# Router logits by column tiles: a batch's four tiles side by side in the array instead of one 512-column product

## The chip, the cores and the metric

The kernel is one program on one core of a Trainium2 chip. It runs four pairs of layers (a cross-attention and a feed-forward layer each) over 4 batches of 512 tokens with 256 features. The metric is the device time of one execution in microseconds (us), from runs of the whole program.

## The reference, cut to what matters

Three of the eight layers are mixtures of experts (layer 0, layer 1 and layer 3). Each begins in the same way: the tokens are normalised, multiplied by a small router matrix, and the two largest of 8 (in layer 1: 7) logits name the token's experts.

```python
x = x + _L0_ffn_ref(_layernorm(x, axis=-1), L0_ffn_router_w, ...)
...
scores = jnp.einsum('btd,de->bte', x, router_w).astype(jnp.float32)      # layer 0: 256 -> 8
probs = jax.nn.softmax(scores, axis=-1)
routing_weights, routing_idx = jax.lax.top_k(probs, TOP_K)
...
logits = xt @ W_router + routing_bias                                    # layer 1: 256 -> 7
probs = jax.nn.sigmoid(logits)
...
logits = xf @ Wg                                                         # layer 3: 256 -> 8
top_w, top_i = jax.lax.top_k(logits, TOP_K)
```

The expert products that follow (gate, up, down for every token and its two experts) are by far the larger work, and the change does not touch them.

## The kernel before, in words

**Names.** P is 128, a tile is 128 tokens, T is 16 tiles, B is 4 batches of TB = 4 tiles (S = 512 tokens). KC = 2 is the number of 128-row pieces of the 256 features. The three expert layers carry the tags e0, e1 and e3.

**Stages.** The program is a row of blocks. In a block each engine has its own queue of instructions, written in the order in which it runs; semaphores order the engines among each other. A block ends for all engines together: nobody begins the next block before the slowest has come to its end, the queue of SyncE (SP) that issues DMAs among them. `experts` opens with two blocks, `normalise` (tags e0n, e1n, e3n) and `route` (e0r, e1r, e3r), and then runs the expert blocks (e0b, e1b, e3b).

**normalise.** VectorE makes mean and inverse deviation of all 16 tiles and then writes the 16 normalised tiles `xn` one after the other (L380; in e1 L383). TensorE turns each tile into a PSUM buffer `tp` of which there are four (L428, two transposes a tile), and ScalarE copies it to `xnT` (L402). Between them stand the router's products. `logits(b)` waits until ScalarE has copied the four tiles of batch b (`copied`), and from b = 2 on until VectorE has copied the logits of batch b - 2 (`lt_copied`), since the PSUM tile `lt` has two buffers. It holds the router's weights (128 x 8) in the array and streams 512 tokens through, once for each of the two pieces of features (L412). In fp32 the profile shows two records for one such product. The order on TensorE is: five filler products, tiles 0 to 5, `logits(0)`, tiles 6 to 9, `logits(1)`, tiles 10 to 13, `logits(2)`, tiles 14 and 15, `logits(3)`, and then `turn_logits` for the four batches (L419). VectorE copies `lt` to `lts` (L390), but those four copies stand behind all 16 `xn` tiles in its queue. `turn_logits(b)` turns 8 x 128 logits for each of the four tiles into `lp`, where tokens lie on the partitions.

**Beside it in the same block.** SP issues loads and stores (`early`, L339): in e0 and e3 the start value of `y_sum` and two pieces of the down weights, in e0 also the rows of a later layer's weights (`rows.load`, L2645 to L2648); in e1 three small matrices.

**route.** It begins with VectorE's copy of `lp` to `lg` (L2040; in e1 an addition of the bias), the search for the two largest (L2043, L2046), and a chain of small operations up to the table `token` (L2158). SP first stores `xn` to `x_rows` (L1976). In e0 the down weights have a left-over half chunk, so POOL clears a part of `xn` (L1818) once two stores of `xn` have landed. In e1 the shared expert's products run on TensorE beside the chain (L1843, L1867), and ScalarE's first silu (L1876) waits for the store of `xn`, whose room it writes. TensorE has filler products (`stay_busy`, L308), 20 and 44 of them in e0 and e3, and 30 at the start of the expert blocks e0b and e3b.

Of the kernel before, what the change touches and what calls it, by code (L numbers as in the profile page):

```python
# [125 lines left out]
def build(nc, ctx, ins, out):  # L126
    def sb(name, shape, dt=F32):
        return ctx.enter_context(nc.sbuf_tensor(name, shape, dt))
# [43 lines left out]
    def matrix(name, n_in, n_out):  # L172
        t = sb(f"w_{name}", [P, n_in // P, n_out])
        loads.append((t[:], ins[name].rearrange("(k p) n -> p k n", p=P)))
        return t
# [50 lines left out]
    for h in range(HC):  # L226
        at = h % 4 * 2 * HD + h // 4 * HD
        loads.append((w.o1[at:at + HD, :, :], o1_rows[h * HD:(h + 1) * HD]))
    w.router = [matrix("L0_ffn_router_w", D, NE), matrix("L1_ffn_W_router", D, NE - 1), matrix("L3_ffn_Wg", D, NE)]
    w.rbias = spread("L1_ffn_routing_bias", NE - 1)  # L230

    w.fm = sb("fm_diag", [P, P])
# [4 lines left out]

    with ExitStack() as st:
        sem = Semaphores(nc, st, "p")
        loaded, made, tr_done, tr_copied, prep = (sem(n) for n in (  # L240
            "loaded", "made", "tr", "trc", "prep"))
        x_in = [sem(f"x{b}") for b in range(B)]
        fm_rows = st.enter_context(nc.sbuf_tensor("fm_rows", [P, HD], F32))
        tp = st.enter_context(nc.psum_tensor("ctx_tp", [P, KC, B * L], F32))
# [1 line left out]
        with nc.Block() as block:  # L246
            FIRST = 6

            @block.sync
            def _(sp):  # L250
                for b in range(B):
                    sp.dma_start(x[:, b * TB:(b + 1) * TB, :], ins["x"][b].rearrange("(t p) d -> p t d", p=P)).then_inc(x_in[b], 16)
                sp.dma_start(consts[:], ins["consts"]).then_inc(loaded, 16)
                sp.dma_start(ctx_load[:], ins["ctx_1024"].rearrange("b l d -> (b l) d")
                             .rearrange("(k p) d -> p k d", p=P)).then_inc(loaded, 16)
                sp.dma_start(ctx_tok[:], ins["ctx_1024"].rearrange("b l d -> l b d")).then_inc(loaded, 16)
                sp.dma_start(w.fmb_row[:], ins["L1_xattn_fm_b"].partition_broadcast(P)).then_inc(loaded, 16)
                sp.dma_start(fm_rows[:], ins["L1_xattn_fm_wT"]).then_inc(loaded, 16)
                sp.dma_start(w.fmb[:], ins["L1_xattn_fm_b8"]).then_inc(loaded, 16)

                for dst, src in loads[0:first_loads]:
                    sp.dma_start(dst, src).then_inc(weights_loaded[0], 16)

            @block.vector
            def _(dve):
# [44 lines left out]
    def normalise(tag, x, xn, rms_weight=None, router=None, stats=None, stats_of_xn=None, arriving=None, early=(), rows=None):  # L310
# [6 lines left out]
        with ExitStack() as st:  # L317
# [8 lines left out]
            idle = st.enter_context(nc.psum_tensor(f"{tag}_idle", [P, S], F32))  # L326
            if router is not None:
                lp, wr, E = router
                lt = [st.enter_context(nc.psum_tensor(f"{tag}_lt{j}", [E, S], F32)) for j in range(2)]
                lts = st.enter_context(nc.sbuf_tensor(f"{tag}_lts", [E, B, S], F32))  # L330
                lt_made, lt_copied = sem("lt_made"), sem("lt_copied")
            with nc.Block() as block:
                if arriving is not None or early:
# [71 lines left out]
                def _(pe):  # L405
                    def logits(b):

                        pe.wait_ge(copied, (b + 1) * TB)
                        if b >= 2:
                            pe.wait_ge(lt_copied, b - 1)  # L410
                        for k in range(KC):
                            last = nc.tensor.matmul(lt[b % 2][:], wr[:, k, :], xnT[:, k, b * S:(b + 1) * S],  # L412
                                                    start=(k == 0), stop=(k == KC - 1))
                        last.then_inc(lt_made, 1)

                    def turn_logits(b):
                        pe.wait_ge(lt_copied, b + 1)
                        for t in range(TB):
                            nc.tensor.transpose(lp[:, b * TB + t, 0:E], lts[:, b, t * P:(t + 1) * P], ident[0:E, 0:E])  # L419

                    if stats_of_xn is None:
                        stay_busy(idle[:], 5 if stats is not None else 16)
# [1315 lines left out]
    def experts(tag, layer, x, wr, w_gate, w_up, w_down, F, rms_weight=None, shared=None, bias=None, outer=None,  # L1738
# [14 lines left out]
        with ExitStack() as st:  # L1753
# [7 lines left out]
            if shared:  # L1761
                NB = (TOP * B * S + E * (P - 1)) // P
                with ExitStack() as s2:
# [6 lines left out]
                    with ExitStack() as s3:  # L1770
                        beside_route = SharedExpert(s3, f"{tag}s", *shared, F, into, fills, kept)
                        with ExitStack() as s4:
                            lp = s4.enter_context(nc.psum_tensor(f"{tag}_lp", [P, T, NE], F32))
                            normalise(f"{tag}n", x, xn, rms_weight, (lp, wr, E), st6, early=beside_route.weights)
                            route(tag, lp, E, wt, slot, owner, token, bias, x, outer, beside_route)
                    kept_blocks(tag, kept_gu, kept_d, (kept, 16 * len(fills[0] + fills[1])), F, NB, E, owner, token)
            else:
                plan = SummedBlocks(st, tag, x, w_down, F, E)
                with ExitStack() as s2:
                    lp = s2.enter_context(nc.psum_tensor(f"{tag}_lp", [P, T, NE], F32))  # L1780
                    normalise(f"{tag}n", x, xn, rms_weight, (lp, wr, E), st6, early=plan.early, rows=beside)
                    route(tag, lp, E, wt, slot, owner, token, bias, x, outer, plan=plan)
                blocks(tag, w_gate, w_up, F, NB, E, owner, token, plan, beside, result)
# [110 lines left out]
    def route(tag, lp, E, wt, slot, owner, token, bias, x, outer, beside=None, plan=None):  # L1894
# [5 lines left out]
        with ExitStack() as st:  # L1900
# [35 lines left out]
            with nc.Block() as block:  # L1936
# [94 lines left out]
                def _(dve):  # L2031
# [4 lines left out]
                    if bias is not None:  # L2036
                        nc.vector.tensor_tensor(lb[:, :, 0:E], lp[:, :, 0:E], bcast(bias[:], 1, T), ALU.add).then_inc(lg_done, 1)
                        dve.wait_ge(prob_done, 1)
                    else:
                        nc.vector.tensor_copy(lg[:], lp[:]).then_inc(lg_done, 1)  # L2040
                        dve.wait_ge(lg_done, 1)
                    for t in range(T):
                        nc.vector.max(m8[:, t, :], lg[:, t, :]).then_inc(max_done, 1)  # L2043
# [1133 lines left out]
```

## Time and profile before

| what | value |
|---|---|
| median of 3 runs | 1805.71 us (1800.82 to 1808.09) |
| the profiled execution's own time | 1800.69 us |
| its span, first to last instruction | 1798.8 us |
| granted TensorE clock, mean over the span | 0.946 of full speed |
| block e0n, from VectorE's first instruction to SP's first in route | 133.2 to 150.9 us |
| block e1n | 934.1 to 951.6 us |
| block e3n | 1474.3 to 1492.1 us |

A row of a time line reads: start, length of the group from its first start to its last end, engine, line, operation, what it writes and reads, shapes, count, and in brackets how long the engine was idle before it and who released it. PE is TensorE, PEld its weight loads, DVE VectorE, ACT ScalarE, POOL GpSimd, SPq the queue that issues DMAs. A matmul record's length holds the time to drain, so records of a stream overlap.

### The profile page before, as it was taken

Reading aid. Unit: us, or ns where it says so; the run is one execution under the profiler, and the core shown is the slowest. Engines: PE = TensorE matmul, PEld = TensorE weight load, DVE = VectorE, ACT = ScalarE, POOL = GpSimd, SP = SyncE. Lnnn points to the kernel's source line nnn. Section 1 sums busy time; section 2 is a strip of 40 time slices with the busy share of each in tenths; the row PEclk is TensorE's granted clock in tenths of the full one; section 3 lists DMA queues with packets and bytes.
Section 4 is the critical chain, followed back from the end, with each engine's and each line's share of the span. In section 5 each row is a group of like instructions: output and inputs, shape, how many; then the busy total and the mean of one; then the engine's idle time right before and its main releaser. Section 6 shows DMA issues by size and latency. Waiting matters only on the chain. (4 is left out here: it accounts for less than half of the span.)

```text
span 1798.8 us, 33336 instructions
## 1 busy us (share of the span) xinstructions
PE 1550.2 (86%) x11830; PEld 1155.5 (64%) x11831; DVE 958.4 (53%) x2462; ACT 487.2 (27%) x1029; POOL 486.0 (27%) x594
## 2 busy tenths in 40 slices
PE   5887999999979986999979899578897888988885
PEld 3653899999858742455444566346665654878785
DVE  4455244444359866766556333689885464222221
ACT  2331111011067531455621122223322431000000
POOL 0101344444400001111102343422120102455543
PEclk9998999999969998999999999788998998999998
DMA  4108677777510017244115133200000025666665
GB/s 142 40 8 277 221 226 223 218 212 222 154 50 2 2 36 194 61 108 111 52 32 170 50 88 82 62 24 13 1 1 1 2 62 189 206 200 201 200 182 140
DMA packets 128641, 200.84 MB, mean 112 GB/s; under 512 B 20368, under 2 KB 77968, under 8 KB 128336
## 3 DMA queue, kind: packets, MB, share of 16 engines
q1 hardware_dynamic: 107696, 169.65, 29.3%
q0 software_dynamic: 20832, 29.68, 8.4%
q8 instruction: 71, 1.16, 0.3%
q14 instruction: 42, 0.34, 0.1%
HBM read 166.21 MB, written 35.16 MB: 112 GB/s over the span
## 5 line engine op out<-in xcount | busy, mean ns | idle before, releaser
L1528 DVE TENSOR_REDUCE l1a_nm<-l1a_sc 128x1 f32<-128x512 f32 (+3 forms) x256 | 107.1, 482 | 53.7 <-PE l1a_sc L1664 53.7
L2271 PEld LDWEIGHTS e0b_gp<-e0b_xT,e0b_wgu 128*128 128x128 f32 x936 | 110.5, 192 | 4.2 <-issue 1.5
L2271 PE MATMUL e0b_gp<-e0b_xT,e0b_wgu 128*128 128x128 f32 x936 | 111.0, 275 | 1.9 <-DVE e0b_hT L2350 1.4
L2331 ACT ACTIVATE e0b_sg<-e0b_gp 128x640 f32<-128x640 f32 x78 | 33.5, 481 | 270.9 <-PE e0b_gp L2271 270.9
L2242 POOL DMA_INDIRECT y_sum<-e0b_yb,e_token x39 | 63.5, 1628 | 145.6 <-DVE e0b_yb L2358 142.5
L2271 PE MATMUL e0b_up<-e0b_xT,e0b_wgu 128*128 128x128 f32 x780 | 93.5, 275 | 0.0
L2242 POOL DMA_INDIRECT y_sum<-e3b_yb,e_token x39 | 63.0, 1617 | 102.2 <-DVE e3b_yb L2358 99.3
L2271 PEld LDWEIGHTS e0b_up<-e0b_xT,e0b_wgu 128*128 128x128 f32 x780 | 90.2, 192 | 0.0
L2331 ACT ACTIVATE e3b_sg<-e3b_gp 128x512 f32<-128x512 f32 x39 | 23.3, 597 | 236.2 <-PE e3b_gp L2271 236.2
L2271 PE MATMUL e3b_up<-e3b_xT,e3b_wgu 128*128 128x128 f32 x624 | 80.3, 285 | 0.0
L2271 PEld LDWEIGHTS e3b_gp<-e3b_xT,e3b_wgu 128*128 128x128 f32 x624 | 75.6, 192 | 3.5 <-issue 0.9
L2271 PE MATMUL e3b_gp<-e3b_xT,e3b_wgu 128*128 128x128 f32 x624 | 76.1, 275 | 1.0 <-DVE e3b_xT L2343 0.5
L2271 PEld LDWEIGHTS e3b_up<-e3b_xT,e3b_wgu 128*128 128x128 f32 x624 | 76.9, 201 | 0.0
L1662 PE MATMUL l1a_sc<-l_stack_k,l_stack_q 128*128 128x512 bf16 (+3 forms) x256 | 59.1, 309 | 16.9 <-PEq L1310 15.2
L2438 PE MATMUL e1b_gu<-e_kgu,e1b_xT 128*128 x152 | 71.7, 594 | 1.7 <-DVE e1b_xT L2502 1.7
L2343 DVE COPY e3b_xT<-e3b_xp 128x256 f32<-128x256 f32 x39 | 16.5, 424 | 95.4 <-PE e3b_xp L2265 95.4
L1662 PEld LDWEIGHTS l1a_sc<-l_stack_k,l_stack_q 128*128 128x128 bf16 x256 | 25.3, 99 | 61.0 <-issue 27.1
L2350 DVE TENSOR_TENSOR e0b_hT<-e0b_up,e0b_sg 128x640 f32<-128x640 f32 x39 | 32.1, 824 | 57.6 <-PE e0b_up L2271 57.6
L1417 POOL TENSOR_TENSOR xn<-xn 128x512 f32<-128x512 f32 x8 | 10.1, 1260 | 194.9 <-DVE xn L1372 183.4
L2350 DVE TENSOR_TENSOR e3b_hT<-e3b_up,e3b_sg 128x512 f32<-128x512 f32 x39 | 27.0, 691 | 61.8 <-PE e3b_up L2271 61.8
L2594 POOL TENSOR_TENSOR f_hq<-f_q,f_q 128x704 f32<-128x704 f32 x16 | 22.9, 1433 | 136.8 <-DVE f_q L2581 136.8
L1191 DVE TENSOR_REDUCE a_nm<-a_sc 128x8 f32<-128x512 f32 x64 | 39.7, 682 | 36.3 <-PE a_sc L1041 36.3
(619 smaller groups left out, 3755.9 us busy)
## 6 DMA issues: line engine op xcount, KB each, us to landing
e3b_wgu<-in_L_ffn_W SPq DMA_DIRECT2D x78, 512.0 KB, 4.6
e0b_wgu<-in_L_ffn_gate_proj SPq DMA_DIRECT2D x39, 704.0 KB, 4.3
e0b_wgu<-in_L_ffn_up_proj SPq DMA_DIRECT2D x39, 704.0 KB, 5.6
x_rows<-xn SPq DMA_DIRECT2D x3, 2048.0 KB, 8.6
l_parts<-l1p_split SPq DMA_DIRECT2D x16, 384.0 KB, 3.1
l_stack_k<-l_parts SPq DMA_DIRECT2D x48, 128.0 KB, 2.7
l_stack_q<-l_parts SPq DMA_DIRECT2D x48, 128.0 KB, 3.0
y_slots<-e1b_yb SPq DMA_DIRECT2D x38, 128.0 KB
```

Of the source, the lines that this page charges most:

```text
L1191: nc.vector.tensor_reduce(nm[:, :, r, :], bank[r][:].rearrange("p t (h l) -> p t h l", l=L), AX_X, ALU.max, negate=True).then_inc(max_done, 1)
L1417: nc.gpsimd.tensor_tensor(whole[n], t1[n], t2[n], ALU.add).then_inc(done, 1)
L1528: nc.vector.tensor_reduce(nm[:, g % 2, q, i:i + 1], sc[q], AX_X, ALU.max, negate=True).then_inc(max_done, 1)
L1662: nc.tensor.matmul(sc[q], of_head(1, n)[:, q * P:(q + 1) * P], of_head(0, n)[:, 0:(q + 1) * P], start=True, stop=False)
L2242: pool.indirect_dma_start(y_sum, bass.IndirectOffsetOnAxis(ap=token[:, n:n + 1], axis=0), yb[n % 2][:], None, compute_op=ALU.add).then_inc ...
L2271: last = nc.tensor.matmul(dst[:, f, :], wgu[j][:, k, at + f * P:at + (f + 1) * P], xT[j][:, k, :], start=(k == 0), stop=(k == KC - 1))
L2331: last = nc.scalar.activation(sg[rows, chunks, :], gp[rows, chunks, :], ACT.Silu)
L2343: nc.vector.tensor_copy(xT[j][:], xp[:]).then_inc(x_copied, 1)
L2350: last = nc.vector.tensor_tensor(hT[j][rows, chunks, :], from_up, sg[rows, chunks, :], ALU.mult)
L2438: last = nc.tensor.matmul(gu[n % 2][:], xT[n % 2][:, k, :], wgu[:, bass.ds(e, 1), k, :].rearrange("p a f -> p (a f)"), start=(k == 0), sto ...
L2594: nc.gpsimd.tensor_tensor(v3(dst), v3(a[:, 0:n]), bcast(sc[:, 0:n // FP4_BLOCK], 2, FP4_BLOCK), ALU.mult).then_inc(result, 1)
```

## The change

The router's weights lie in tiles of 32 columns, whose columns 8 to 31 (7 to 31 in layer 1) are cleared once by POOL in the program's first block. `logits(b)` gives each of the batch's four tiles a column group of the array of its own: for each piece of features, four products of 128 x 32 weights by 128 tokens, which write 32 partitions each of one PSUM tile [128, 128]. VectorE's copy is then 128 x 128 instead of 8 x 512, and one transpose turns all four tiles of a batch. `lp` is 32 columns wide for a tile, and `route` reads the first 8 (7).

```diff
-    w.router = [matrix("L0_ffn_router_w", D, NE), matrix("L1_ffn_W_router", D, NE - 1), matrix("L3_ffn_Wg", D, NE)]
+    ROUTER = P // TB
+    w.router = []
+    for name, n_out in (("L0_ffn_router_w", NE), ("L1_ffn_W_router", NE - 1), ("L3_ffn_Wg", NE)):
+        w.router.append(sb(f"w_{name}", [P, KC, ROUTER]))
+        loads.append((w.router[-1][:, :, 0:n_out], ins[name].rearrange("(k p) n -> p k n", p=P)))
...
+            @block.gpsimd
+            def _(pool):
+                for router in w.router:
+                    nc.gpsimd.memset(router[:], 0.0).then_inc(cleared, 1)
+                pool.wait_ge(cleared, len(w.router))
...
-                lt = [st.enter_context(nc.psum_tensor(f"{tag}_lt{j}", [E, S], F32)) for j in range(2)]
-                lts = st.enter_context(nc.sbuf_tensor(f"{tag}_lts", [E, B, S], F32))
+                lt = [st.enter_context(nc.psum_tensor(f"{tag}_lt{j}", [P, P], F32)) for j in range(2)]
+                lts = st.enter_context(nc.sbuf_tensor(f"{tag}_lts", [P, B, P], F32))
...
                         for k in range(KC):
-                            last = nc.tensor.matmul(lt[b % 2][:], wr[:, k, :], xnT[:, k, b * S:(b + 1) * S],
-                                                    start=(k == 0), stop=(k == KC - 1))
+                            for t in range(TB):
+                                at = (b * TB + t) * P
+                                last = nc.tensor.matmul(lt[b % 2][t * ROUTER:(t + 1) * ROUTER, :], wr[:, k, :], xnT[:, k, at:at + P],
+                                                        start=(k == 0), stop=(k == KC - 1))
                         last.then_inc(lt_made, 1)
...
-                        for t in range(TB):
-                            nc.tensor.transpose(lp[:, b * TB + t, 0:E], lts[:, b, t * P:(t + 1) * P], ident[0:E, 0:E])
+                        nc.tensor.transpose(lp[:, b * TB:(b + 1) * TB, :].rearrange("p t e -> p (t e)"), lts[:, b, :], ident)
...
-                            lp = s4.enter_context(nc.psum_tensor(f"{tag}_lp", [P, T, NE], F32))
+                            lp = s4.enter_context(nc.psum_tensor(f"{tag}_lp", [P, T, ROUTER], F32))
...
-                        nc.vector.tensor_copy(lg[:], lp[:]).then_inc(lg_done, 1)
+                        nc.vector.tensor_copy(lg[:], lp[:, :, 0:NE]).then_inc(lg_done, 1)
```

On TensorE, in the block e3n (e0n and e1n read alike), the queue of before holds these rows; `e3n_tp` are the turned tiles, `e3n_lt` the logits with the experts on the partitions, `e_lp` those with the tokens on the partitions. A row counts products here, not the profile's records.

```order
L308 MATMUL e3n_idle<-ones_h,ident_h 128x512 x5
L428 MATMUL e3n_tp<-consts,xn 128x128 x12
L412 MATMUL e3n_lt<-xnT,w_L_ffn_Wg 8x512 x2
L428 MATMUL e3n_tp<-consts,xn 128x128 x8
L412 MATMUL e3n_lt<-xnT,w_L_ffn_Wg 8x512 x2
L428 MATMUL e3n_tp<-consts,xn 128x128 x8
L412 MATMUL e3n_lt<-xnT,w_L_ffn_Wg 8x512 x2
L428 MATMUL e3n_tp<-consts,xn 128x128 x4
L412 MATMUL e3n_lt<-xnT,w_L_ffn_Wg 8x512 x2
L419 MATMUL e_lp<-consts,e3n_lts 128x8 x16
```

The same place in the queue of the changed kernel (its lines are numbered some ten higher):

```order
L318 MATMUL e3n_idle<-ones_h,ident_h 128x512 x5
L439 MATMUL e3n_tp<-consts,xn 128x128 x12
L424 MATMUL e3n_lt<-xnT,w_L_ffn_Wg 32x128 x8
L439 MATMUL e3n_tp<-consts,xn 128x128 x8
L424 MATMUL e3n_lt<-xnT,w_L_ffn_Wg 32x128 x8
L439 MATMUL e3n_tp<-consts,xn 128x128 x8
L424 MATMUL e3n_lt<-xnT,w_L_ffn_Wg 32x128 x8
L439 MATMUL e3n_tp<-consts,xn 128x128 x4
L424 MATMUL e3n_lt<-xnT,w_L_ffn_Wg 32x128 x8
L430 MATMUL e_lp<-consts,e3n_lts 128x128 x4
```

Nothing has moved in the order: each group of 2 products with 512 columns has become 8 with 128 columns on 32 partitions, and the 16 small transposes at the end are 4 full ones.

On VectorE, at the end of the same block and the start of route, the queue of before holds:

```order
L376 RECIPROCAL e3n_rstd<-e3n_root 128x16
L380 TENSOR_SCALAR xn<-x,e3n_mean,e3n_rstd 128x256 x16
L390 COPY e3n_lts<-e3n_lt 8x512 x4
L332 UNCONDITIONAL_BRANCH
L2030 UNCONDITIONAL_BRANCH
L2033 MEMSET e3k_weight_of 128x2
L2040 COPY e3r_lg<-e_lp 128x128
```

and in the changed kernel:

```order
L386 RECIPROCAL e3n_rstd<-e3n_root 128x16
L390 TENSOR_SCALAR xn<-x,e3n_mean,e3n_rstd 128x256 x16
L400 COPY e3n_lts<-e3n_lt 128x128 x4
L342 UNCONDITIONAL_BRANCH
L2041 UNCONDITIONAL_BRANCH
L2044 MEMSET e3k_weight_of 128x2
L2051 COPY e3r_lg<-e_lp 128x128
```

The four copies of the logits keep their place behind the 16 tiles of `xn`; only their shape is another.

## Rows read from the trace of the kernel before

**Rows 1.** The page: busy time of each engine, and POOL in 40 slices.

```profile
PE 1550.2 (86%) x11830; PEld 1155.5 (64%) x11831; DVE 958.4 (53%) x2462; ACT 487.2 (27%) x1029; POOL 486.0 (27%) x594
...
POOL 0101344444400001111102343422120102455543
```

**Rows 2.** Time line of block e3n: start, us, engine, line.

```profile
1476.25 5.25 DVE L380 TENSOR_SCALAR xn<-x,e3n_mean,e3n_rstd 128x256 f32<-128x256 f32 x16
1476.71 2.82 PE L428 MATMUL e3n_tp<-consts,xn 128*128 128x128 f32 x12 [1.09 <-DVE xn L380]
...
1479.46 2.19 PE L412 MATMUL e3n_lt<-xnT,w_L_ffn_Wg 128*8 128x512 f32 x4
...
1485.75 1.88 PE L412 MATMUL e3n_lt<-xnT,w_L_ffn_Wg 128*8 128x512 f32 x4
...
1487.57 0.66 PE L428 MATMUL e3n_tp<-consts,xn 128*128 128x128 f32 x4
...
1488.74 1.88 PE L412 MATMUL e3n_lt<-xnT,w_L_ffn_Wg 128*8 128x512 f32 x4 [0.52 <-ACT xnT L402]
...
1490.56 1.25 PE L419 MATMUL e_lp<-consts,e3n_lts 8*128 8x8 f32 x16
1490.66 0.68 DVE L390 COPY e3n_lts<-e3n_lt 8x512 f32<-8x512 f32 x1 [2.31 <-PE e3n_lt L412]
1492.06 0.37 SPq L1976 DMA_DIRECT2D x_rows<-xn  x1
```

**Rows 3.** Time line of block e1n.

```profile
936.42 6.42 DVE L383 SCALAR_TENSOR_TENSOR xn<-inner,e1n_rstd,s_L_ffn_w_ln 128x256 f32<-128x256 f32 x16
...
947.15 0.66 PE L428 MATMUL e1n_tp<-consts,xn 128*128 128x128 f32 x4
...
948.33 1.88 PE L412 MATMUL e1n_lt<-xnT,w_L_ffn_W_router 128*7 128x512 f32 x4 [0.52 <-ACT xnT L402]
...
951.64 0.37 SPq L1976 DMA_DIRECT2D x_rows<-xn  x1
```

**Rows 4.** Time line of TensorE in layer 0's attention, 66 to 72 us.

```profile
68.09 1.17 PE L1041 MATMUL a_sc<-a_kd,a_qT 32*128 32x128 f32 x32
69.20 1.07 PE L1075 MATMUL a_ob<-a_pT,a_vd 128*32 128x256 f32 x16
70.09 1.06 PE L1083 MATMUL a_rb<-a_pT,consts 128*32 128x128 f32 x32
```

**Rows 5.** Stretches of e0n and e0r: busy time, granted clock, DMA share, GB/s.

```profile
145.00:148.00 3.00, 2.48 (x9) 0.69 (x8) 0.68 (x1) 0.76 (x3) 0.00 (x0) 1.00 1.09 350
...
163.00:166.00 3.00, 3.00 (x16) 1.37 (x14) 3.00 (x2) 0.00 (x0) 0.00 (x0) 1.00 1.09 347
```

**Rows 6.** SP's queue around the end of block e0n.

```profile
148.32 0.37 SPq L2648 DMA_DIRECT2D f2w_rows<-in_L_ffn_w_down  x1
150.91 0.37 SPq L1976 DMA_DIRECT2D x_rows<-xn  x1
```

**Rows 7.** Waits of e0n and e0r, the longest.

```profile
POOL xn L1818 <- DMA x_rows<-xn: 32.5, 1, 32.5
```

**Rows 8.** Time line of e3r and the start of e3b.

```profile
1492.14 0.29 DVE L2040 COPY e3r_lg<-e_lp 128x128 f32<-128x128 f32 x1
...
1497.96 9.66 PE L308 MATMUL e3r_idle<-ones_h,ident_h 128*128 128x512 bf16 x44
...
1514.85 0.18 DVE L2158 CAST e_token<-e3r_row_f 128x39 uint32<-128x39 f32 x1
...
1515.34 9.46 PE L308 MATMUL e3b_gp<-ones_h,ident_h 128*128 128x512 bf16 x30 [1.74 <-PEq L1936]
```

**Rows 9.** A stretch of e3r, with columns as in rows 5.

```profile
1507.00:1510.00 3.00, 0.62 (x3) 0.10 (x1) 3.00 (x2) 0.00 (x0) 3.00 (x2) 1.00 0.01 4
```

**Rows 10.** Time line of TensorE in e1r: products of the shared expert.

```profile
955.20 3.60 PE L1843 MATMUL e1s_up<-xnT,e1s_wu 128*128 128x512 f32 x8
961.32 5.37 PE L1843 MATMUL e1s_gp<-xnT,e1s_wg 128*128 128x512 f32 x8 [2.52 <-ACT xn L1876]
```

More of the change, by code:

```diff
@@ L239, in build @@
         sem = Semaphores(nc, st, "p")
-        loaded, made, tr_done, tr_copied, prep = (sem(n) for n in (
-            "loaded", "made", "tr", "trc", "prep"))
+        loaded, made, tr_done, tr_copied, prep, cleared = (sem(n) for n in (
+            "loaded", "made", "tr", "trc", "prep", "cleared"))
         x_in = [sem(f"x{b}") for b in range(B)]
@@ L1779, in experts @@
                 with ExitStack() as s2:
-                    lp = s2.enter_context(nc.psum_tensor(f"{tag}_lp", [P, T, NE], F32))
+                    lp = s2.enter_context(nc.psum_tensor(f"{tag}_lp", [P, T, ROUTER], F32))
                     normalise(f"{tag}n", x, xn, rms_weight, (lp, wr, E), st6, early=plan.early, rows=beside)
```

## The prediction

> **What bounds the kernel now.** I read the page first: TensorE is busy 86% of the span and no other engine over 53% [rows 1]. That is a mean over stages, so it says little about three blocks of under 18 us each. The time line of a block says more, and the reader is to follow who waits for whom in it.
>
> In e3n VectorE is through with its 16 tiles at 1476.25 + 5.25 = 1481.50, but the block ends at 1492.06. Behind VectorE the block is a chain of TensorE and ScalarE with one period a batch: from `logits(2)` (1485.75) to the next transposes (1487.57) 1.82 us, from there to `logits(3)` (1488.74) 1.17 us, which is two tiles turned and copied by ScalarE. Then comes a tail: products 1.88 us, VectorE's copy 0.68 us from 1490.66 to 1491.34, and 0.72 us of the last transposes and the end of the block [rows 2]. e1n runs in the same way, only that its `xn` tiles take 6.42 us, up to 942.84 [rows 3].
>
> e0n looks the same on TensorE, but two other things happen there. SP issues its last DMA of the block at 148.32 and is done at 148.69, 2.2 us ahead of the block's end [rows 6]; and the DMA engines are full, share 1.09, in a stretch inside e0n and in one 18 us later in e0r [rows 5]. What e0r waits for in the end is a landing: POOL stands 32.5 us until the stores of `xn` have landed [rows 7].
>
> **What the new products cost.** The trace of before holds the nearly exact form: L1083, 128 x 32 weights by 128 columns in fp32, four column groups in turn, 32 records in 1.06 us [rows 4]. A batch's logits are now 8 products, 16 records. Half of 1.06 is 0.53 us; with the last record's drain, which does not halve, I take 0.60 us until the next work of another form starts and 0.65 us until VectorE has the result. The bounds: below, 0.53; above, no overlap of the groups at all, which leaves the 1.82 us of before, since the same columns stream. I stay near the lower end, for the row differs from the new products only in its operands. The 64 weight loads a stage instead of 16 are inside that row, since it has one for each record too.
>
> Changing between full and column-tiled products happens eight times a stage. The row: L1041 uses the array as four row groups, starts at 68.09 and runs 1.17 us, to 69.26; L1075, in column groups, starts at 69.20 [rows 4]. So a change of form waits for hardly more than the last record, and 0.60 holds that. The Trainium skill (TensorEngine Tiling (Array Packing), Key Properties) says that changing the mode drains the array; by that rule, read as a start 0.06 us later at each of 8 changes, a stage would lose 0.5 us more, the sum would be 9.4 us and the time 1796.3; the row does not show that extra.
>
> VectorE's copy: 8 x 512 takes 0.68 us [rows 2], and a 128 x 128 copy out of PSUM takes 0.29 us [rows 8]. The bounds are these two; I take 0.29, as it is the same form, a gain of 0.39 us, which counts once a stage, for the last batch. Turning: three of the four transposes are done while VectorE copies the last batch, and one is left instead of four small ones. Of the 0.72 us after the copy I let 0.1 go.
>
> **e3n.** Three times 1.82 - 0.60, once 1.88 - 0.65, then 0.39 and 0.1: 3.66 + 1.23 + 0.49 = 5.4 us. The first `logits` took 2.19 instead of 1.88 us at a clock not yet up [rows 2]; the new ones meet the same clock, so I book nothing there. Does VectorE become the bound? `logits(2)` needs the copy of batch 0, which comes at 1481.50 + 0.29 = 1481.8. TensorE reaches it at about 1479.46 + 2 x (0.6 + 1.17) + 0.3 = 1483.3, later, so no. After the block VectorE's chain in route ends at 1514.85 + 0.18 and the next block starts at 1515.34 [rows 8]; the DMA engines are idle in 1507 to 1510, share 0.01 [rows 9], so the stores landed early enough to move 5.4 us forward. e3n pays in full.
>
> **e1n.** Here VectorE is later. Last `xn` tile 942.84, copy of batch 0 to 943.13, `logits(2)` from 943.2 to 943.8, transposes to `logits(3)` 948.33 - 947.15 = 1.18 us, so 944.98; then 0.65 for products, 0.35 for the copy with its handover, 0.6 for the turn and the end: 946.6 instead of 951.64 [rows 3]. The gain is 5.0 us. In e1r TensorE is the bound apart from one wait of 2.52 us before its second gate product, which hangs on the store of `xn` [rows 10], and that store is the first DMA of the block, so it moves too.
>
> **e0n.** The block could end 2.2 us earlier, where SP stands. But the two stores of `xn`, behind which POOL waits, stand in a full DMA queue whose bytes are the same and which was full before and after [rows 5, 7]. They land when they did. I take 0; the other bound is the 2.2 us.
>
> **The rest.** POOL's three fills of 128 x 64 lie in the first slice of the program, where POOL has nothing to do (digit 0) [rows 1]; uncovered, at the 0.29 us of a copy of 128 elements [rows 8], they would be 0.9 us. `route` reads `lp` with gaps instead of in one piece, 128 elements in both cases, so its 0.29 us [rows 8] stay. SP's loads of the routers are the same pieces.
>
> **Sum.** 5.0 + 5.4 + 0 = 10.4 us. The profiled execution took 1800.69 us, so it would take 1790.3. That execution is near the lowest of the runs shown, whose median is 1805.71, and I forecast the median: 1795.3 us.
>
> **Rivals.**
> - *The clock takes a part back.* e3b opens with 30 filler products that took 9.46 us, while 44 of the same took 9.66 us in e3r [rows 8], so 0.22 us each at full clock and, at half, 0.44. Those 30 could take 6.6 us or 13.1 us, depending on when the clock rises. If the earlier start meets the worse case, 3.6 us go: gain 6.8, time 1798.9. For it: nothing sets when the clock rises but TensorE's activity, and that shifts. Against: the better case, 2.9 us more gain, is as open; both are in the own range.
> - *e0n pays too*: 2.2 us more, 12.6, time 1793.1. For it: the block's end is visibly TensorE's. Against: the share of 1.09.
> - *The column groups do not overlap here*, as the accumulation over two pieces might make each wait. Then only copy and turn are left, 0.5 us in each of two stages: 1.0, time 1804.7. Against: L1083 adds up four products in one place of PSUM as well, and keeps its pace [rows 4].
> - *The other side, slower: TensorE stays at half clock* through e1n and e3n and into the next stages, because the new products keep it less busy. Twelve transposes took 2.82 us at the low clock, so 1.9 us for eight; with 1.2 us for logits and 0.3 of ScalarE a batch takes 3.4 us instead of 2.99. The stage gains nothing and loses 1 us with the tail, twice 1.0; in e1r gate and up at half clock cost 2 x 3.60 less the wait of 2.52 [rows 10], 4.7 us; the filler 3.6 us. Together 10.3 us slower, 1816.0. It decides once the low clock lasts through the tail of both stages, which takes all 10.4 us of gain. Against: in e3n the low clock ended by itself under transposes alone, before the second batch, and eight transposes in every 1.8 us keep the array at work for most of it. The Trainium skill (TensorE: Matmul & The Clock Gate, Part 1) says that the throttled state is the default and activity lifts it; that would speak for this rival only if the array stood still for long, and no row of e3n shows that.
>
> **Chances and range.** Forecast 0.58; clock takes back 0.17; e0n pays 0.10; no overlap 0.10; slower 0.05. A difference of 0.5%, 9.0 us, is about what a measurement of this kernel tells from no change, so the line is 1796.7 us, close to the forecast. Of the forecast's case two thirds lie below it, of the second a sixth, of the third nearly all: 0.39 + 0.03 + 0.10 = 0.52 faster. Slower by over 0.5% is most of the last rival, 0.04; the rest, 0.44, is the same. The likeliest case's own range is 1791 to 1799 (the filler either way). The range for all is 1788.5 to 1803: it takes in the first three cases and the spread of the runs before, and leaves out the last two.
>
> **What would show it.** Right: L424's 16 records a batch within 0.7 us; e3n ends 5 to 6 us after its last `xn` tile instead of 10.6, e1n under 4 us after instead of 8.8; VectorE's copies 0.29 us; POOL's L1818 ends its wait at the same distance from the block's start. Wrong, if the logits' records follow each other at over 0.1 us, if the granted clock in 937 to 947 or after 1480 falls to 0.5, if the span from e3n's end to the first expert product grows, or if e0's POOL wait ends earlier.

## The result, and the profile after

| what | before | changed |
|---|---|---|
| median, runs on one chip | 1800.86 us (1799.31 to 1808.09, 5 runs) | 1788.0 us (1782.94 to 1790.93, 5 runs) |
| ratio, with its 95% interval | | 0.9911 (0.9882 to 0.9940) |
| the profiled execution's span | 1798.8 us | 1789.0 us |
| e0n / e0r | 17.5 / 28.2 us | 15.6 / 29.7 us |
| e1n / e1r | 17.5 / 49.9 us | 13.3 / 48.2 us |
| e3n / e3r | 17.5 / 23.2 us | 12.0 / 22.3 us |
| e3b, from its first product to the issue of the last store of the result | 274.6 us | 274.4 us |

The change is faster by 0.9%: 0.0089 x 1800.86 = 16.0 us, 10.8 to 21.3 by the interval. That ratio is worked out from all runs and is not the ratio of the two medians, which differ by 12.9 us. The forecast was 10.4 us and 1795.3 us; the measured median, 1788.0 us, is 0.5 us below its range of 1788.5 to 1803. A block is counted here between the same early instruction of it and of the next one (the first that touches `e0n_m`, `e0r_idle` and so on), so e0n and e3n come out some 0.25 us shorter than from first instruction to first.

In the page of the changed kernel TensorE has 15.1 us less to do than in [rows 1], and its share of the span is the same.

```profile
PE 1535.1 (86%) x11938; PEld 1155.7 (65%) x11939; DVE 954.2 (53%) x2462; ACT 487.7 (27%) x1029; POOL 487.1 (27%) x597
```

**e3n**, time line of the changed kernel, to be held against [rows 2]:

```profile
1473.34 5.26 DVE L390 TENSOR_SCALAR xn<-x,e3n_mean,e3n_rstd 128x256 f32<-128x256 f32 x16
1473.80 2.82 PE L439 MATMUL e3n_tp<-consts,xn 128*128 128x128 f32 x12 [1.10 <-DVE xn L390]
...
1476.55 0.92 PE L424 MATMUL e3n_lt<-xnT,w_L_ffn_Wg 128*32 128x128 f32 x16
...
1480.33 0.64 PE L424 MATMUL e3n_lt<-xnT,w_L_ffn_Wg 128*32 128x128 f32 x16
...
1480.90 0.66 PE L439 MATMUL e3n_tp<-consts,xn 128*128 128x128 f32 x4
...
1482.08 0.64 PE L424 MATMUL e3n_lt<-xnT,w_L_ffn_Wg 128*32 128x128 f32 x16 [0.52 <-ACT xnT L412]
...
1482.65 0.81 PE L430 MATMUL e_lp<-consts,e3n_lts 128*128 128x128 f32 x4
1482.79 0.29 DVE L400 COPY e3n_lts<-e3n_lt 128x128 f32<-128x128 f32 x1 [1.46 <-PE e3n_lt L424]
...
1483.72 0.37 SPq L1987 DMA_DIRECT2D x_rows<-xn  x1
```

The 16 records of a batch take 0.64 us where 1.88 stood, and the next transposes start 0.57 us after the first of them (1480.33 to 1480.90). VectorE's copy is 0.29 us instead of 0.68, and SP's first store of route comes 1483.72 - 1478.60 = 5.12 us after the last `xn` tile, where it was 10.56.

**e1n**, against [rows 3]:

```profile
939.04 6.42 DVE L393 SCALAR_TENSOR_TENSOR xn<-inner,e1n_rstd,s_L_ffn_w_ln 128x256 f32<-128x256 f32 x16
...
942.25 1.08 PE L424 MATMUL e1n_lt<-xnT,w_L_ffn_W_router 128*32 128x128 f32 x16
...
943.27 1.77 PE L439 MATMUL e1n_tp<-consts,xn 128*128 128x128 f32 x8
...
944.97 0.64 PE L424 MATMUL e1n_lt<-xnT,w_L_ffn_W_router 128*32 128x128 f32 x16
...
946.71 0.64 PE L424 MATMUL e1n_lt<-xnT,w_L_ffn_W_router 128*32 128x128 f32 x16
...
950.10 0.37 SPq L1987 DMA_DIRECT2D x_rows<-xn  x1
```

Here eight transposes take 1.77 us instead of 1.09, and the first logits 1.08 instead of 0.64: the granted clock is low in the first two batches, at 0.50 (1.2 GHz) in these 2 us:

```profile
942.00:944.00 2.00, 2.00 (x22) 1.33 (x21) 2.00 (x6) 0.69 (x3) 0.00 (x0) 0.50 0.04 8
```

The prediction had named a clock of 0.5 in this place as a sign of being wrong. It did come, and it is not the change's doing alone: the kernel before has it in some of its profiles too (below, `before_again`). The block ends 4.64 us after the last `xn` tile (939.04 + 6.42 = 945.46), not under 4 as forecast.

**e1r.** TensorE's time line behind that block, against [rows 10], and the granted clock of 3 us in which the second gate product begins, in the changed kernel:

```profile
953.65 3.60 PE L1854 MATMUL e1s_up<-xnT,e1s_wu 128*128 128x512 f32 x8
959.80 3.70 PE L1854 MATMUL e1s_gp<-xnT,e1s_wg 128*128 128x512 f32 x8 [2.55 <-ACT xn L1887]
```

```profile
core 0: us, PE busy (x) PEld busy (x) DVE busy (x) ACT busy (x) POOL busy (x), PEclk, DMA share, GB/s
959.00:962.00 3.00, 2.20 (x5) 1.06 (x6) 2.86 (x10) 0.75 (x2) 0.47 (x1) 1.00 1.09 365
```

and the same place in the kernel before:

```profile
961.00:964.00 3.00, 2.68 (x3) 1.18 (x4) 2.70 (x10) 0.26 (x1) 0.02 (x1) 0.55 1.09 361
```

The wait is the same, 2.55 and 2.52 us. The eight records behind it take 3.70 us at a clock of 1.00, 2.4 GHz, where they took 5.37 with 0.55 granted, nearly all of it the lower level. That is 1.67 us of gain in a block that the change does not touch.

**e3r** has the same thing in small. The last products of its chain, in the changed kernel and then before:

```profile
1503.01 1.30 PE L1977 MATMUL e3r_small<-e3r_numbers,e3r_place_hot 128*128 128x78 bf16 x32 [3.73 <-DVE e3r_numbers L2137]
```

```profile
1511.34 2.26 PE L1966 MATMUL e3r_small<-e3r_numbers,e3r_place_hot 128*128 128x78 bf16 x32 [3.72 <-DVE e3r_numbers L2126]
```

0.96 us less behind a wait of the same length. The granted clock around these products, in the changed kernel and then before:

```profile
1503.00:1504.00 1.00, 0.99 (x28) 0.99 (x29) 0.00 (x0) 0.00 (x0) 0.00 (x0) 1.00 0.00 0
1504.00:1505.00 1.00, 0.31 (x9) 0.17 (x5) 0.65 (x7) 0.00 (x0) 0.00 (x0) 0.74 0.00 0
```

```profile
1510.00:1511.00 1.00, 0.00 (x0) 0.00 (x0) 1.00 (x2) 0.00 (x0) 0.49 (x1) 0.92 0.00 0
1511.00:1512.00 1.00, 0.66 (x11) 0.66 (x12) 0.28 (x1) 0.00 (x0) 0.00 (x0) 0.50 0.00 0
```

In the kernel before the clock has fallen when the products begin. In the changed kernel it falls as well, but only when they are nearly done: the fall was moved, not avoided.

**e0.** SP's queue around the end of e0n and POOL's wait, against [rows 6, 7]:

```profile
148.91 0.37 SPq L2659 DMA_DIRECT2D f2w_rows<-in_L_ffn_w_down  x1
149.68 0.37 SPq L1987 DMA_DIRECT2D x_rows<-xn  x1
```

```profile
POOL xn L1829 <- DMA x_rows<-xn: 32.1, 1, 32.1
```

The block now ends where SP is done and is 1.9 us shorter, and e0r takes 1.5 us more: given back, as forecast. POOL's wait ends 35.4 us behind SP's first instruction of e0n before (168.57 - 133.16) and 35.1 us behind it now (168.96 - 133.85).

### The profile page after: what moved, and what is told of

It is laid out like the page before. It is cut to its first block and busy times, and to the rows that moved or that the text cites. A ratio compares the mean times of both kernels' runs of the same rounds, so it can differ in the third digit from the quotient of the medians.

```text
span 1789.0 us, 33557 instructions
## 1 busy us (share of the span) xinstructions
PE 1535.1 (86%) x11938; PEld 1155.7 (65%) x11939; DVE 954.2 (53%) x2462; ACT 487.7 (27%) x1029; POOL 487.1 (27%) x597
## 5 line engine op out<-in xcount | busy, mean ns | idle before, releaser
L1202 DVE TENSOR_REDUCE a_nm<-a_sc 128x8 f32<-128x512 f32 x64 | 39.8, 684 | 37.1 <-PE a_sc L1052 37.1
```

Of the source, the lines that this page charges most:

```text
L1202: nc.vector.tensor_reduce(nm[:, :, r, :], bank[r][:].rearrange("p t (h l) -> p t h l", l=L), AX_X, ALU.max, negate=True).then_inc(max_done, 1)
```

## The experiments

Each ratio is against the kernel before on the same chip (17 or 23 runs of it, medians 1803.73 to 1803.95 us). It comes from all runs, so it can differ from the ratio of the medians by up to 0.0013 (`one_group`). The gain is (1 - ratio) x 1803.9, with its interval. "Blocks" is what one profile of the kernel shows in the six blocks, e0n, e0r, e1n, e1r, e3n and e3r, against the mean of the profiles with untiled products in that stage: e0n + e0r 45.8 us, e1n 18.3, e1r 50.1, e3n 17.4, e3r 23.2. Those means are from six or seven profiles each. The mean of e1r holds the 51.6 us of `one_group`; the other five lie at 49.7 to 49.9.

| kernel | median us | ratio (interval) | gain us | blocks us |
|---|---|---|---|---|
| `again` | 1787.84 | 0.9905 (0.9885 to 0.9924) | 17.1 (13.7 to 20.7) | 14.2 |
| `only_e0` | 1799.83 | 0.9983 (0.9968 to 0.9997) | 3.1 (0.5 to 5.8) | 0.4 |
| `only_e1` | 1792.51 | 0.9941 (0.9922 to 0.9960) | 10.6 (7.2 to 14.1) | 7.2 |
| `only_e3` | 1790.98 | 0.9931 (0.9913 to 0.9949) | 12.4 (9.2 to 15.7) | 6.9 |
| `one_group` | 1804.92 | 0.9994 (0.9979 to 1.0008) | 1.1 (-1.4 to 3.8) | -2.3 |
| `two_groups` | 1794.88 | 0.9959 (0.9941 to 0.9976) | 7.4 (4.3 to 10.6) | 7.8 |
| `moved_before` | 1807.83 | 1.0012 (0.9999 to 1.0026) | -2.2 (-4.7 to 0.2) | 0.4 |
| `moved_after` | 1787.45 | 0.9900 (0.9880 to 0.9919) | 18.0 (14.6 to 21.6) | 19.9 |
| `before_fill` | 1802.30 | 0.9992 (0.9977 to 1.0008) | 1.4 (-1.4 to 4.1) | 2.5 |
| `early_copy` | 1787.65 | 0.9922 (0.9894 to 0.9949) | 14.1 (9.2 to 19.1) | 14.9 |
| `best` | 1784.18 | 0.9891 (0.9864 to 0.9919) | 19.7 (14.6 to 24.5) | 20.8 |

**The change once more (`again`), and the tiles in one layer alone.** The theory: the gain is made of e1n and e3n with what lies right behind them, and e0 pays nothing. The rival: e0 pays too, or there is a gain elsewhere. `only_e1`, `only_e0` and `only_e3` differ in the list:

```diff
+                tiled = tag in ['e1n']
...
+                        for k in range(KC if not tiled else 0):
+                            last = nc.tensor.matmul(lt[b % 2][:], wr[:, k, 0:E], xnT[:, k, b * S:(b + 1) * S],
+                                                    start=(k == 0), stop=(k == KC - 1))
+                        for k in range(KC if tiled else 0):
```

> The changed kernel once more, beside new runs of the kernel before. Theory A (the change is worth the 9.6 us that the two profiles show in e1 and e3, the rest of the measured difference is the chance of when TensorE's clock rises): 9 to 12 us faster, ratio near 0.994. Theory B (there is a further gain that the profiles of one run each did not show): 14 to 18 us faster, ratio near 0.991, as before.

> Column tiles in layer 0's router alone, layers 1 and 3 as before (with the padded weights read in 8 columns). Theory A: no gain, within 1 us, since the stores of xn in e0 wait in a full DMA queue; the block e0n ends where SP does, near 15.8 us after its start. Theory B: 2 to 5 us faster, if the shorter block is worth something after all.

> Column tiles in layer 1's router alone. Theory A: 5.0 us faster (the block e1n 13.4 to 12.5 us long instead of 17.5, and all of it passed on). Theory B: more than 5, since e1r is bound by TensorE and may find a higher clock: 6 to 8 us.

> Column tiles in layer 3's router alone. Theory A: 5.4 us faster (block e3n 12.3 us instead of 17.7). Theory B: more, through e3r and the fillers at the start of e3b, 7 to 9 us.

e1n goes to 13.3 us and e1r to 48.2 in `only_e1`, and e1r is at 49.7 and 49.9 in the other two; e3n goes to 12.0 and e3r to 22.3 in `only_e3` and in neither of the other two. So each effect sits behind its own stage. `only_e0` has e0n + e0r at 45.2 us, a gain of 0.6, though its runs put it at 3.1 us (0.5 to 5.8). By the runs all four came out above the theory A of their expectation, and `only_e1` and `only_e3` above theory B as well, while the blocks of `only_e1` and `only_e3` (7.2 and 6.9 us) are near what their theory B named, a gain in e1r and e3r. The three gains add to 26.1 us, and the whole change gives 17.1. Part of this is that the three share one measurement of the kernel before, part is the stage at the end. Granted clock over the 240 us that begin 10 us after e3b's start, in the kernel before, in `again` and in `only_e3`:

```profile
1525.30:1765.30 240.00, 208.75 (x1530) 197.85 (x1531) 57.69 (x109) 22.09 (x37) 126.01 (x107) 0.98 0.67 196
```

```profile
1516.90:1756.90 240.00, 209.84 (x1562) 198.72 (x1563) 58.73 (x110) 22.09 (x37) 127.10 (x108) 0.99 0.69 199
```

```profile
1520.50:1760.50 240.00, 211.37 (x1586) 200.27 (x1587) 59.85 (x112) 22.69 (x38) 129.09 (x109) 1.00 0.69 202
```

From e3b to the end these took 274.6, 270.2 and 268.9 us. Over all fourteen profiles this stretch lies between 268.9 and 275.5 us: 272.3 to 275.5 (mean 274.5) for the five kernels without overlapping groups in any layer, 270.2 to 275.2 (mean 272.2) for the five with four groups in all three, 272.8, 269.2 and 268.9 in `only_e0`, `only_e1` and `only_e3`, and 275.4 in `two_groups`. So a single profile is uncertain by some 3 us here. The first pair of profiles differed by only 9.8 us, although their six blocks differ by 12.7, and this stretch is not the reason. What stands ahead of e3b outside the six blocks, which the change does not touch, took 1361.5 us in the first profile of the kernel before, the least of all fourteen, and 1364.9 in the changed kernel (1368.7 in `moved_before`). The pair was unlucky for the change there; its own profiled execution was the slowest of five. Whether the tiles move this clock a little on the average is open; even the lower end of the interval of `only_e3` is 2.3 us above what its blocks explain.

**A second profile of the kernel before (`before_again`)**, without a change.

> The kernel before once more, for a second profile of it. Theory A+ (part of the gain is in stretches behind the changed blocks, at TensorE's clock): the gate product of e1r behind the wait for the store takes 5.2 to 5.4 us again and the last products of e3r 2.3 us, as in the three profiles with an unchanged block there, and the expert blocks e3b take 270 to 280 us at random. Rival (those were chance): the two durations differ from profile to profile.

```profile
940.23 2.73 PE L428 MATMUL e1n_tp<-consts,xn 128*128 128x128 f32 x12 [1.59 <-DVE xn L383]
942.88 3.13 PE L412 MATMUL e1n_lt<-xnT,w_L_ffn_W_router 128*7 128x512 f32 x4
```

The first logits took 3.13 us instead of 1.88 and e1n 19.0 instead of 17.5. The product in e1r behind the wait took 5.26 us and the last ones of e3r 2.26, as theory A+ had it. Its time was 1802.68 us, its e3b stretch 272.3. Over seven profiles with untiled e1n that block took 17.5 (three times), 18.7, 18.9, 19.0 and 19.2 us: the block which the prediction read was at the lucky end.

**All products on one column group (`one_group`).** The theory: the gain is the overlap of the groups. The rival: padding or shorter products bring it. The edit also runs tile by tile, with the two pieces of features inside, and makes `lt` and `lts` 32 x 512:

```diff
...
-                                last = nc.tensor.matmul(lt[b % 2][t * ROUTER:(t + 1) * ROUTER, :], wr[:, k, :], xnT[:, k, at:at + P],
+                                last = nc.tensor.matmul(lt[b % 2][:, t * P:(t + 1) * P], wr[:, k, :], xnT[:, k, at:at + P],
...
-                        nc.tensor.transpose(lp[:, b * TB:(b + 1) * TB, :].rearrange("p t e -> p (t e)"), lts[:, b, :], ident)
+                        for t in range(TB):
+                            nc.tensor.transpose(lp[:, b * TB + t, :], lts[:, b, t * P:(t + 1) * P], ident[0:ROUTER, 0:ROUTER])
```

> The same 128 x 32 by 128 products as in the change, with the same padded weights, but all four tiles of a batch on the same 32 columns of the array, one after the other; copy is 32 x 512 and four transposes turn a batch. Theory A (the gain is the overlap of the four column groups): no overlap, a batch's logits take 1.8 us again and the time is that of before, 0 to 2 us slower. Rival (shorter products or narrower weights are what pays): 8 us or more faster, as the change.

```profile
1488.37 1.93 PE L424 MATMUL e3n_lt<-xnT,w_L_ffn_Wg 128*32 128x128 f32 x16
1490.24 1.09 PE L440 MATMUL e3n_tp<-consts,xn 128*128 128x128 f32 x8
```

The same 16 records take 1.93 us, and the next transposes start 1.87 us behind the first of them; e3n is at 17.4 us and by the runs there is no gain. Padding and shorter products bring nothing. VectorE's copy is 0.68 us again here (32 x 512), so the run does not part the overlap from the smaller copy, which comes with it; by the rows the copy is 0.39 us of the 5.4, and the rest is the overlap and one transpose instead of four. (The -2.3 us in the column of blocks are the clock in this one profile, in e1n with 19.2 us and in e1r with 51.6.)

**Two column groups (`two_groups`)** asks whether the gain is in proportion. The `lt` and `lts` tiles are 64 x 256 in it.

```diff
...
-                            for t in range(TB):
-                                at = (b * TB + t) * P
+                        for u in range(2):
+                            for k in range(KC):
+                                for g in range(2):
+                                    at = (b * TB + u * 2 + g) * P
...
```

> The batch's four tiles on two column groups instead of four, two tiles after each other in each; the copy is 64 x 256 and two transposes turn a batch. Theory A (the overlap of the column groups is what pays): records follow each other at 0.055 us instead of 0.027 or 0.113, a batch's logits take 1.0 us, the block e3n is 3.5 us shorter than before instead of 5.4, and the whole time lies between: 8 to 12 us faster than before. Rival (a drain at the change of form is what the block loses now): no better than two thirds of that.

```profile
1482.68 1.07 PE L425 MATMUL e3n_lt<-xnT,w_L_ffn_Wg 128*32 128x128 f32 x16
1483.67 1.09 PE L442 MATMUL e3n_tp<-consts,xn 128*128 128x128 f32 x8
```

From the logits to the next transposes it is 0.99 us: 1.87, 0.99, 0.57 for one, two and four groups. The way to the next work is thus about 0.14 us plus 1.73 us divided by the number of groups (estimate from the three). e1n and e3n both took 13.9 us, and the whole is 7.4 us faster, just under the 8 to 12 expected: the overlap fits, and the rival's price for a change of form does not show. And the clock behind them fell as in the kernel before: the gate product behind its wait of 2.60 us took 5.40 us, e1r 50.0, e3r 23.2. Shorter e1n and e3n do not bring the gain downstream by themselves: e3n is 3.5 us shorter here and e3r as long as before, where with four groups it is 5.4 and e3r pays.

**The later rows' loads moved out of e0n (`moved_before`, `moved_after`).** The theory: e0 pays nothing because SP's queue and the DMA engines behind it are full; without the five loads the change's gain shows in e0 as well. The rival: e0 is held by something else, or the loads cost the kernel before by themselves. Either edit, on the kernel before and on the changed one:

```diff
-                        if rows is not None:
-                            rows.load(sp)
...
                     load_gate_up(0, 0)
                     load_gate_up(1, 1)
+                    if rounds is not None:
+                        rounds.load(sp)
                     step(0, 0)
```

> The kernel before, with the five loads of a later layer's weight rows taken out of e0n's DMA queue and issued at the start of e0b. Theory A (in e0 the stores of xn wait in a full DMA queue): they land some 6 us sooner, e0r is 24 to 25 us instead of 28.2, so 3 to 5 us faster less what the loads cost in e0b (0 to 2). Rival (the queue was not what e0r waits for): no change, or slower by the loads' time in e0b.

> The changed kernel with the same five loads moved. Theory A: now e0n pays its 5.4 us too, so the distance to the version with loads moved and without column tiles is that of the change plus 5, and this is the fastest version, near 1780 us. Rival (e0n's gain is lost to something else): the distance is the same as without the move.

Stage e0n + e0r took 45.2 us in `moved_before`, where POOL still waits 31.5 us, and 39.8 in `moved_after`, where it waits

```profile
POOL xn L1827 <- DMA x_rows<-xn: 26.1, 1, 26.1
```

So e0n pays its 5.4 us once the five loads are gone. But the expectation for `moved_before` was wrong: the stores did not land 6 us sooner, and e0r took 27.9 us, not 24 to 25. Its DMA engines were all but idle when route began (its first store is issued at 151.85):

```profile
150.00:153.00 3.00, 2.70 (x23) 1.68 (x23) 1.73 (x14) 1.15 (x1) 0.00 (x0) 1.00 0.07 24
```

POOL was released 17.1 us behind that first store all the same, against 17.7 before, 19.3 in the changed kernel and 16.8 in `moved_after`. Most of that time is therefore the transfers of route itself, the second store of `xn` being issued behind a load of down weights. What the five loads cost is the end of the block, through SP's queue, and 2.5 us of landing once the block is shorter. These are two effects, and no run parts them: `moved_after` takes both away.

`moved_after` is 20.4 us below `moved_before` by the medians, where the change (`again`) is 16.1 below the kernel before. That is 4.3 of the 5 us more that were expected, on intervals of some 3 us either way. Against the change itself it is level (1787.45 against 1787.84 and 1788.0), and far from the 1780 expected, although its profiled execution, 1778.96 us, was its fastest; its runs spread up to 1792.02. The gain in the block is shown, its worth in the median is not.

**Filler in the wait of e1r (`before_fill`).** The theory: what e1r gains is the clock behind the wait, so ten filler products in that wait give it to the kernel before as well. The rival: e1r gains because a transfer lands earlier.

```diff
                             beside.gate(pe, b)
                             beside.up_product(pe, b)
+                            if b == 0:
+                                stay_busy(beside.yp[1][:].rearrange("p t d -> p (t d)"), 10)
```

> The kernel before with ten filler products of 128 x 512 in bf16 in e1r, where TensorE waits 2.5 us for the store of xn. Theory A+ (in the kernel before TensorE's clock falls over that wait and the changed kernel escapes it): the gate product behind it takes 3.7 instead of 5.3 us, e1r is 48.2 instead of 49.9 us with no column tiles, 1.7 us faster as a whole, within what can be measured. Rival (the 1.7 us come from something else that the column tiles do): e1r stays at 49.7 to 49.9 us.

```profile
962.48 2.32 PE L308 MATMUL e1s_yp<-ones_h,ident_h 128*128 128x512 bf16 x10
965.23 3.70 PE L1843 MATMUL e1s_gp<-xnT,e1s_wg 128*128 128x512 f32 x8 [0.43 <-ACT xn L1876]
```

The product takes 3.70 us and e1r 48.2, exactly as in the changed kernel, with nothing else touched. So the length of that product is the clock's. That is 1.9 us of the 2.5 in the table; the rest is mostly an e1n of 17.5 us that met a high clock. But the next stage, which the table leaves out, gave it back. The first expert product of e1b, here and in the kernel before:

```profile
1009.42 3.65 PE L2440 MATMUL e1b_gu<-e_kgu,e1b_xT 128*128 x4 [0.71 <-DVE e1b_xT L2504]
```

```profile
1007.08 1.98 PE L2438 MATMUL e1b_gu<-e_kgu,e1b_xT 128*128 x4 [0.75 <-DVE e1b_xT L2502]
```

It took 1.98 us in all thirteen other profiles and 1.67 more in this one, as much as the filler had won in e1r: the fall of the clock came one block later. By the runs 1.4 us are won with an interval that holds zero, so the run shows the cause in e1r and not a gain of the whole.

**VectorE copies batch 0 among the tiles (`early_copy`).** The theory: in e1n `logits(2)` waits for a copy behind all `xn` tiles, as the prediction had it. The rival: TensorE is late anyway.

```diff
+                        if router is not None and t == 11:
+                            dve.wait_ge(lt_made, 1)
+                            nc.vector.tensor_copy(lts[:, 0, :], lt[0][:]).then_inc(lt_copied, 1)
-                    for b in range(B if router is not None else 0):
+                    for b in range(1, B if router is not None else 0):
```

> The changed kernel with VectorE's copy of the first batch's logits moved ahead of the last four tiles of xn. Theory A (in e1n the third batch's logits wait for that copy): e1n 12.5 us instead of 13.1 to 13.3, e3n the same as it was TensorE's, the whole 0.5 us faster than the change, not to be told apart. Rival (the low clock after the first tiles sets e1n's length): e1n stays at 13.1 to 13.3.

```profile
944.30 0.65 PE L427 MATMUL e1n_lt<-xnT,w_L_ffn_W_router 128*32 128x128 f32 x16
...
946.05 0.64 PE L427 MATMUL e1n_lt<-xnT,w_L_ffn_W_router 128*32 128x128 f32 x16
...
947.80 0.64 PE L427 MATMUL e1n_lt<-xnT,w_L_ffn_W_router 128*32 128x128 f32 x16
```

The batches follow at 1.75 us each and e1n took 12.1 us. In `moved_after`, where the clock was up in e1n too but the copies stand behind the tiles, `logits(2)` came 2.07 us behind `logits(1)` and the block took 12.5:

```profile
937.02 0.64 PE L422 MATMUL e1n_lt<-xnT,w_L_ffn_W_router 128*32 128x128 f32 x16
...
938.65 0.49 DVE L398 COPY e1n_lts<-e1n_lt 128x128 f32<-128x128 f32 x2
939.09 0.64 PE L422 MATMUL e1n_lt<-xnT,w_L_ffn_W_router 128*32 128x128 f32 x16 [0.41 <-ACT xnT L410]
```

The bracket names ScalarE, but the first of VectorE's two copies, begun at 938.65 and some 0.29 us long, ends just before 939.09, and `early_copy` takes 0.32 us of this wait away (2.07 to 1.75). So VectorE is the bound when the clock is up, and it is worth those 0.32 us. In the profiles of the change as it is (13.3 and 13.1 us) and of `only_e1` (13.3), the low clock was. Most of the step from 13.1 to 12.1 us is thus that the clock was up in this profile, not the edit.

**All together (`best`)**: the tiles, the moved loads, the early copy and the filler, by the diffs above.

> Column tiles, with the five loads moved to e0b, the early copy and the filler in e1r together. Theory A: e0n and e0r together 39.8 us instead of 45.2 as in the version with the loads moved, the rest as the parts showed, so 6 us faster than the change: near 1782. Rival (what e0 gives is lost again behind it, as the medians of the version with moved loads suggest): near 1787.

e0n + e0r took 39.3 us, e1n 12.1, e1r 48.2, e3n 12.1, e3r 22.3. The filler adds nothing to the tiles: e1r takes 48.2 us without it too. Its median of 1784.18 us is the lowest of the study and lies between the 1782 expected and the rival's 1787. Against the change (1787.84 and 1788.0 elsewhere) it is some 3.7 us, and the intervals of the two ratios overlap.

## Why the prediction missed low

The forecast gain was too small and the forecast time too high.

- **The overlap of the groups** (0.60 and 0.65 us a batch): right. 0.57 and 0.64 us were measured, `one_group` shows that neither padding nor shorter products bring it, and the change of form costs nothing beyond the forecast.
- **e3n, 5.4 us**: right, from 17.3 to 17.5 us in the seven untiled profiles to 11.9 to 12.1 in the six with four groups.
- **e0, nothing**: right in the size. The block gained 1.9 us, of the 2.2 that SP's queue allowed, and e0r gave 1.5 of them back. That POOL's release does not move was right too (35.4 and 35.1 us). The cause was told too simply: most of POOL's wait is route's own transfers, as `moved_before` shows, and the five loads add 2.5 us only when the block is shorter.
- **e1n, 5.0 us**: right in the gain, not in the two lengths. The forecast's 12.5 us is what `moved_after` took, with VectorE as the bound. The change took 13.3 and 13.1 because of a low clock, and the kernel before took 18.3 on the average because of the same. The difference is 5.1 us.
- **"In e1r TensorE is the bound apart from one wait ..., that store is the first DMA of the block, so it moves too"**: the step that failed. It moved the block and left its length as it was. The row beside it [rows 10] held a product of 5.37 us next to equal ones of 3.60, a penalty of the clock behind the wait, and the sum booked nothing for its going; it stood only in the rival on the slower side, as a price to be paid more often. With four groups it went, 1.7 us in the rows and 1.9 us in the block (1.6 without the profile of `one_group`). e3r repeats it with 0.95 us. Together 2.6 to 2.9 us were missing from the sum.
- **Sum.** By blocks the change and its repeat gain 0.6 + 5.1 + 1.9 + 5.4 + 0.9 = 13.9 us, where 10.4 were forecast. 13.9 lies inside the intervals of both comparisons, 16.0 (10.8 to 21.3) and 17.1 (13.7 to 20.7), with 2 to 3 us unexplained. The means of the e3b stretch differ by as much (274.5 and 272.2), but single profiles of either kind overlap, so no run assigns it.
- **The base.** The forecast subtracted from a median of three runs, 1805.71 us. In the five runs beside the change its median was 1800.86, and comparisons with 17 and 23 runs put it at 1803.7 to 1804.0. The forecast time was 7.3 us too high. Against the five runs 4.85 us of this are the base and 2.45 the gain (12.86 between the medians, 10.4 forecast); against the longer comparisons 1.8 are the base and 5.5 the gain. That the time fell below the range, by 0.5 us, needed both.
- **Rivals.** The clock did change something downstream, but gave instead of taking: the filler at the start of e3b took 9.13 to 9.55 us in every profile (9.46 in [rows 8], 9.22 after), never 6.6 or 13.1. The queue of TensorE alone does not set the clock: e1n of one and the same kernel took 17.5 and 19.0 us. No overlap and half clock did not come.

Why the clock holds over a wait of 2.5 us in six profiles with four groups in e1n, one of them with filler in the wait, and falls in all seven of the others without filler is not settled. `two_groups` rules out that any shortening does it, and `before_fill` shows only what it costs. In e3r of the changed kernel and in e1b of `before_fill` the fall came later and not never. The Trainium skill (TensorE: Matmul & The Clock Gate, HAM oscillation) says that a wait can throttle the clock so that the work behind it starts cold; the 5.37 us in the kernel before agree with that, and the 3.70 us behind the same wait show that the wait's length alone does not decide.

## What to carry to other kernels

Four products with 32 output columns each, side by side in the array, took a third of the time that they take one after the other (0.64 against 1.93 us): look for rows with a narrow output (`128*8`), and size the new form by a row of the same shape that the kernel already has. When a block is shortened, look behind it twice: at the queues that hold its end (here the loads in SP's queue took the gain back until they were moved away), and at equal products of unequal length behind a wait, since the clock behind the wait can change when the work ahead of it does. Follow such a gain into the stages behind: in `before_fill` it was lost again one block later. Before a gain under 1% is forecast from one profile, a second profile of the same kernel tells which of its rows are luck; here e1n differed by 1.5 us and the last stage by 2.3 between two profiles of the kernel before.

## What the runs showed of the hardware

- Column groups overlap though they accumulate over two pieces: 16 records of 128 x 32 by 128 columns in fp32 take 1.93 us on one group, 1.07 on two, 0.64 to 0.65 on four. The Trainium skill (TensorE: Matmul & The Clock Gate, Part 3) gives 2.38 times for three column tiles; here the way to the next work shrank 1.87 / 0.57 = 3.3 times for four.
- The granted clock fell or held over waits of one length: behind 2.5 to 2.6 us of waiting, eight equal records took 3.70 or 5.1 to 5.4 us (in `one_group`, behind 2.9 us, 6.7), and behind 3.7 us of waiting 32 records took 1.30 or 2.26 us.
- The last 270 us of the program, 87 to 88% busy on TensorE, vary by 6.6 us between profiles, with a mean granted clock of 0.97 to 1.00.
- POOL was released 16.8 to 17.7 us behind the first store of `xn` in three kernels, whether the DMA engines were idle before it (0.07) or full (1.09), and 19.3 us behind it in the changed one.
